# Attention visits in pairs of one window, with the score weighting on ScalarE and the one-hot made by one operation per visit

## The reference

```python
h = relu(layernorm(x))                       # x [12500, 64]
lin_x = h @ W_lin.T + b_lin
feat = concat([h[src], edge_attr, h[dst]])   # 144 per edge
scores = relu(feat @ W_att1.T + b_att1) @ W_att2.T + b_att2
m = segment_max(scores, src)                 # per source node
e = exp(scores - m[src])
denom = segment_sum(e, src)
msg = segment_sum(e / denom[src] * lin_x[dst], src)
# then a gated update (sigmoid, sigmoid, tanh) of every node with an edge
```

## Time and profile before

| what | us |
|---|---|
| median of three runs (lowest, highest) | 6971.01 (6955.53, 6972.53) |
| the profiled execution | 6953.3 |
| its span | 6951.5 |
| row send, first start of line 832 to last | 2519.9 to 4770.8 |
| attention, first C_N to the first operation after it | 4801.04 to 6833.62 |

### The profile page before, as it was taken

The page is one execution under the profiler, slowest core; times in us unless marked ns, Lnnn a source line. Parts: engine busy times, 40 slices in busy tenths (PEclk is TensorE's granted clock), DMA queues, the critical chain, the costliest instruction groups (busy, mean ns, idle before and its releaser), DMA issues.

```text
span 6951.5 us, 172751 instructions
## 1 busy us (share of the span) xinstructions
PE 4916.4 (71%) x30025; PEld 3702.1 (53%) x30026; DVE 4522.2 (65%) x20036; ACT 2115.2 (30%) x5541; POOL 4929.4 (71%) x10449
## 2 busy tenths in 40 slices
PE   6444777777545766676666666666888888888887
PEld 2334444444434544455445444444777777777775
DVE  5777888888434743333333333335999999999997
ACT  4000000000000432222222222223555555555555
POOL 1677777777777367777777777776777777777775
PEclk9555555555555777767877787776888888888888
DMA  8333333333333143333333333334333333333333
GB/s 270 67 60 60 57 60 60 57 60 60 64 60 61 62 133 111 111 110 109 105 106 105 106 106 105 106 105 128 95 94 94 95 95 95 94 94 95 95 95 93
DMA packets 1146496, 649.15 MB, mean 93 GB/s; under 512 B 798450, under 2 KB 1050340, under 8 KB 1145573
## 3 DMA queue, kind: packets, MB, share of 16 engines
q1 hardware_dynamic: 1006804, 412.21, 24.3%
q0 software_dynamic: 137728, 233.30, 11.8%
q10 hardware_dynamic: 1888, 2.83, 0.2%
HBM read 360.75 MB, written 311.42 MB: 97 GB/s over the span
## 4 chain that ended last, share of the span: by engine, by line
issue 19%; PE 15%; POOL 14%; DVE 8%; DMA 4%; ACT 3%; POOLq 1%; DVEq 1%; ACTq 0%; SPq 0%
PE banks L1397 7%; POOL rows_by_src L832 6%; DMA rows_by_src<-ring 3%; PE banks L1443 3%; DVE wide L1991 2%; DVE wide L1996 1%; DVE ring L2002 1%; ACT ring L1085 1%; ACT ring L1092 1%; POOL ring L893 1%; PE banks L1398 1%; PE banks L1385 1%; PE banks L1434 1%; DVE ring L1947 1%; PE banks L1458 1%
## 5 line engine op out<-in xcount | busy, mean ns | idle before, releaser
L832 POOL DMA_INDIRECT rows_by_src<-ring x1760 | 1711.7, 973 | 553.1 <-issue 488.5
L804 POOL DMA_INDIRECT wide<-msg_table,ring x1664 | 1578.8, 949 | 632.1 <-issue 419.4
L1397 PE MATMUL banks<-wide,ring 128*128 x3520 | 1281.9, 492 | 473.6 <-ACT ring L1085 403.4
L1311 PE MATMUL banks<-wide,ring 128*128 x3520 | 859.5, 426 | 505.7 <-DVE acc L1764 190.9
L1397 PEld LDWEIGHTS banks<-wide,ring 128*128 128x128 f32 x3520 | 742.5, 261 | 746.6 <-issue 696.2
L1311 PEld LDWEIGHTS banks<-wide,ring 128*128 128x128 f32 x3520 | 784.7, 328 | 584.0 <-issue 583.5
L1092 ACT COPY ring<-banks 128x416 f32<-128x416 f32 x880 | 402.2, 510 | 1448.8 <-PE banks L1398 1448.8
L1958 DVE COPY ring<-ring 128x4 f32<-128x4 f32 x440 | 80.1, 182 | 1145.5 <-DMA rows_by_src<-ring 1145.4
L1443 PE MATMUL banks<-wide,ring 128*128 x5328 | 708.6, 262 | 0.0
L1764 DVE TENSOR_TENSOR acc<-acc,banks 128x64 f32 x1760 | 388.8, 221 | 366.0 <-DVE acc L1764 201.8
L1443 PEld LDWEIGHTS banks<-wide,ring 128*128 128x128 bf16 x5328 | 544.1, 108 | 114.2 <-issue 0.2
(11 more groups left out here) (326 smaller groups left out, 9426.3 us busy)
## 6 DMA issues: line engine op xcount, KB each, us to landing
wide<-rows_by_src SPq DMA_DIRECT2D x1776, 105.0 KB, 2.0
ring<-attr_turned SPq DMA_DIRECT2D x440, 128.0 KB
attr_turned<-ring SPq DMA_DIRECT2D x416, 96.0 KB
rows_by_src<-ring POOLq DMA_INDIRECT x1760
wide<-msg_table,ring POOLq DMA_INDIRECT x1664
ring<-attr_by_dst SPq DMA_DIRECT2D x208, 64.0 KB
attr_turned<-ring SPq DMA_DIRECT2D x208, 64.0 KB
attr_by_dst<-in_edge_attr_dram SPq DMA_DIRECT2D x1, 13281.2 KB
```

What stands on the lines that cost most here:

```text
L804: g.indirect_dma_start(out=A_g[:, b * GV + u, :], out_offset=None, in_=table[:, :], in_offset=bass.IndirectOffsetOnAxis(ap=A_idx[:, b * GV ...
L832: g.indirect_dma_start(out=rows_d[:, :], out_offset=bass.IndirectOffsetOnAxis(ap=B_pos[:, s, u:u + 1], axis=0), in_=B_row[:, s, u, :], in_ ...
L1311: last = mm(bank[s][:, u * HID:(u + 1) * HID], A_D[:, s, u, :], A_g[:, ds(r[u], 1), :].rearrange("p a k -> p (a k)"), start=True, stop=True)
L1397: mm(b, B_DT[:, t, u, :], qh[:, w, :].rearrange("p a k -> p (a k)"), start=True, stop=False)
```

## The change

In the attention stage, the visits of a window are rounded up to an even number, so that two neighbours in a group of four (a pair) always have the same window. There are then 1,872 visits, 468 ticks, 78 bodies. The maximum, scan, penalty and split of the maximum run on 2 columns a tick, not 4; PE adds the sums of a pair in PSUM, and the DVE adds 2 sums a tick into `acc`, not 4. Penalties are made once ahead of the loop (`pens`), and POOL copies twelve of them each body.

C_N is made without C_kl: one DVE operation per visit adds the window's first node to the node numbers and compares with the edge's source, so four `tensor_scalar` of 128 columns with two per-partition scalars stand for one operation of 512. It stands behind the scan in DVE's tick. C_W goes from POOL (one operation of 260 columns) to ACT (four of 65, with a per-partition scale), behind the exponential. C_S and C_STb go to the end of ACT's tick, the turning of C_N behind the turning of the scores on PE.

In the rows stage, rows outside the window are sent to 2,048 spare rows behind the table, a place of its own for each, and the indirect DMA has no bounds check; the DVE has one small operation more per four visits.

```diff
-C_VISITS = C_BODY * -(-VISITS // C_BODY)
+C_VISITS = C_BODY * -(-(-(-N_EDGES // P) + N_WIN - 1 + N_WIN) // C_BODY)
 C_LOOPS = C_VISITS // C_BODY
-VTAB = max(VISITS, C_VISITS)
+PV = GV // 2
+VTAB = VISITS
 VCHUNK = VTAB // 4
...
-        rows_d = dram("rows_by_src", [SLOTS, ROW])
+        rows_d = dram("rows_by_src", [SLOTS + BODY * P, ROW])
...
-                            in_=B_row[:, s, u, :], in_offset=None, bounds_check=SLOTS - 1, oob_is_err=False).then_inc(b_sc[s], 16)
+                            in_=B_row[:, s, u, :], in_offset=None).then_inc(b_sc[s], 16)
...
-                if 0 in stages:
-                    n = i * C_BODY + s * GV
-                    pool.wait_ge(c_in[s], H0_LOADS[s] + 16 * GV * (i + 1))
-                    after_c(pool, c_N, s, i, CS)
-
-                    g.tensor_tensor(C_kl[:, s, :], C_V[:, s, :, ROW_SRC], wbase[:, ds(n, GV)], ALU.subtract).then_inc(c_kl, 1)
-
-                    m_pen = ch.do(g.tensor_tensor(C_pen[:, s, :], wbase_all[:, ds(n, GV)], wbase[:, ds(n, GV)], ALU.subtract))
+                if 0 in stages and s == 3:
+                        after_c(pool, c_new, CS - 1, i, CS)
+                        g.tensor_copy(C_pen, pens[:, ds(i * (CS * PV), CS * PV)]).then_inc(c_pen, 1)
                 if 2 in stages:
                     t, j = stages[2]
                     sp_ = [C_parts[:, t, k * GV:(k + 1) * GV] for k in range(PARTS)]
                     after_c(pool, c_s, t, j, incs=2)
                     after_c(pool, c_pt, t, j, CS)
-                    m_r = ch.do(g.tensor_tensor(C_r[:, t, :], C_s[:, t, :], sp_[0], ALU.subtract))
-                if 0 in stages:
-                    ch.need(m_pen)
-                    g.tensor_tensor(C_pen[:, s, :], C_pen[:, s, :], C_step, ALU.mult).then_inc(c_pen, 1)
-                if 2 in stages:
-                    ch.need(m_r)
+                    ch.link(g.tensor_tensor(C_r[:, t, :], C_s[:, t, :], sp_[0], ALU.subtract))
                     ch.link(g.tensor_tensor(sp_[1], C_r[:, t, :], C_zero, ALU.add))
                     g.tensor_tensor(sp_[2], C_r[:, t, :], sp_[1], ALU.subtract).then_inc(c_sp, 1)
                 if 4 in stages:
...
-                    after_c(pool, c_p, t, j)
-                    after_c(pool, c_ag, t, j, 2)
-                    g.tensor_tensor(C_W[:, t % 2, :, :], C_V[:, t, :, H1:ROW_SRC],
-                                    per_group(C_p[:, t, :], HID + 1), ALU.mult).then_inc(c_W, 1)
                 if 3 in stages:
                     t, j = stages[3]
...
                     after_c(pool, c_new, t, j)
+                    pool.wait_ge(c_pen, j + 1)
                     after_c(pool, c_mm, t, j, CS)
...
-            run_ticks(pool, tick, 5, ch, CS * (1 + 2 + 1 + 4), CS, C_LOOPS)
+            run_ticks(pool, tick, 5, ch, CS * (2 + 1 + 4), CS, C_LOOPS)
...
-                if 0 in stages:
-                    after_c(act, c_N, s, i)
-                    after_c(act, c_ag, s, i, CS)
-                    a.activation(C_S[:, s, :, :], C_N[:, s, :, :], ACT.Identity, bias=ones[:, 0:1], scale=-1.0).then_inc(c_S, 1)
                 if 4 in stages:
...
                     after_c(act, c_d, t, j)
                     after_c(act, c_W, t, j, CS)
                     a.activation(C_p[:, t, :], C_d[:, t, :], ACT.Exp).then_inc(c_p, 1)
-                if 0 in stages:
-                    after_c(act, c_St, s, i)
-                    after_c(act, c_mm, s, i, CS)
-                    a.activation(C_STb[:, s, :, :], four(bank_b[0], P), ACT.Identity, bias=ones[:, 0:1], scale=-1.0).then_inc(c_STc, 1)
+                    after_c(act, c_p, t, j)
+                    after_c(act, c_ag, t, j, 2)
+                    for u in range(GV):
+                        last = a.activation(C_W[:, t % 2, u, :], C_V[:, t, u, H1:ROW_SRC], ACT.Identity, scale=C_p[:, t, u:u + 1])
+                    last.then_inc(c_W, 1)
                 if 2 in stages:
                     t, j = stages[2]
                     after_c(act, c_pt, t, j)
                     after_c(act, c_MKt, t, j, 2)
                     a.copy(C_PT[0:PARTS * GV, t % 2, :], bank_b[1][0:PARTS * GV, 0:P]).then_inc(c_pc, 1)
+                if 0 in stages:
+                    after_c(act, c_N, s, i, incs=GV)
+                    after_c(act, c_ag, s, i, CS)
+                    a.activation(C_S[:, s, :, :], C_N[:, s, :, :], ACT.Identity, bias=ones[:, 0:1], scale=-1.0).then_inc(c_S, 1)
+                    after_c(act, c_St, s, i)
+                    after_c(act, c_mm, s, i, CS)
+                    a.activation(C_STb[:, s, :, :], four(bank_b[0], P), ACT.Identity, bias=ones[:, 0:1], scale=-1.0).then_inc(c_STc, 1)
...
-                    r = regs(ENG.PE, wwin, j1 * C_BODY + t1 * GV, N_WIN - 1)
+                    r = regs(ENG.PE, wpair_of, j1 * (C_BODY // 2) + t1 * PV, N_WIN - 1, PV)
...
-                        last = mm(bank[5][:, u * PARTS:(u + 1) * PARTS], C_STb[:, t, u, :], C_mp[:, t, u, :], start=True, stop=True)
+                        last = mm(bank[5][:, u * PARTS:(u + 1) * PARTS], C_STb[:, t, u, :], C_mp[:, t, u // 2, :], start=True, stop=True)
...
-                if 0 in stages:
-                    after_c(pe, c_N, s, i)
-                    after_c(pe, c_STc, s, i, 1)
-                    for u in range(GV):
-                        last = tr(bank_b[0][:, u * P:(u + 1) * P], C_N[:, s, u, :], ident_b[:, :])
-                    last.then_inc(c_St, 1)
                 if 1 in stages:
                     after_c(pe, c_STc, t1, j1)
                     after_c(pe, c_add, t1, j1, 1, incs=2)
...
-                        w = p_tab[:, ds(r[u], 1), :].rearrange("p a k -> p (a k)")
+                        w = p_tab[:, ds(r[u // 2], 1), :].rearrange("p a k -> p (a k)")
...
                     after_c(pe, c_pc, t, j, 1)
                     turn(pe, "pe")
                     tr(bank_b[1][0:PARTS * GV, 0:P], C_parts[:, t, :], ident_b[:, :]).then_inc(c_pt, 1)
+                if 0 in stages:
+                    after_c(pe, c_N, s, i, incs=GV)
+                    after_c(pe, c_STc, s, i, 1)
+                    for u in range(GV):
+                        last = tr(bank_b[0][:, u * P:(u + 1) * P], C_N[:, s, u, :], ident_b[:, :])
+                    last.then_inc(c_St, 1)
                 if 5 in stages:
                     t, j = stages[5]
                     after_c(pe, c_W, t, j)
                     after_c(pe, c_acc, t, j, 2)
                     after_c(pe, c_S, t, j)
                     for u in range(GV):
-                        last = mm(bank[6 + t % 2][:, u * (HID + 1):(u + 1) * (HID + 1)], C_S[:, t, u, :], C_W[:, t % 2, u, :],
-                                  start=True, stop=True)
+                        last = mm(bank[6 + t % 2][:, (u // 2) * (HID + 1):(u // 2 + 1) * (HID + 1)], C_S[:, t, u, :], C_W[:, t % 2, u, :],
+                                  start=u % 2 == 0, stop=u % 2 == 1)
                     last.then_inc(c_ag, 1)
...
-                v.tensor_tensor(nt[0:K, :], t1, hs, ALU.mult).then_inc(s_vcols, 1)
+                if k == 0:
+                    v.tensor_tensor(nt[0:K, :], t1, hs, ALU.mult).then_inc(s_vcols, 1)
+                else:
+                    ch.link(v.tensor_scalar(ei, t1, 1.0, None, ALU.add))
+                    ch.link(v.tensor_scalar(ei, ei, 1, None, ALU.arith_shift_right))
+                    ch.link(v.tensor_copy(t1, ei))
+                    v.scalar_tensor_tensor(nt[0:K, :], t1, 2.0, hs, ALU.mult, ALU.mult).then_inc(s_vcols, 1)
...
-                    ch.link(v.scalar_tensor_tensor(B_sh[:, s, :], B_rec[:, s, :, 1], -BIG, B_in[:, s, :], ALU.add, ALU.mult))
+                    ch.link(v.tensor_tensor(B_sh[:, s, :], B_rec[:, s, :, 1], aside[:, s, :], ALU.subtract))
+                    ch.link(v.tensor_tensor(B_sh[:, s, :], B_sh[:, s, :], B_in[:, s, :], ALU.mult))
                     if not first(i):
                         dve.wait_ge(b_sc[s], 16 * GV * i)
                     v.tensor_copy(B_row[:, s, :, ROW_SRC], B_rec[:, s, :, 0]).then_inc(b_pos, 1)
-                    v.tensor_scalar(B_pos[:, s, :], B_sh[:, s, :], BIG, None, ALU.add).then_inc(b_pos, 1)
+                    v.tensor_tensor(B_pos[:, s, :], B_sh[:, s, :], aside[:, s, :], ALU.add).then_inc(b_pos, 1)
...
-            v.memset(C_step, MASKED / P).then_inc(c_init, 1)
+            dve.wait_ge(c_init, N_CINIT - 1)
+            ch.link(v.tensor_tensor(pens, of_pairs(wbase_all[:, 0:C_VISITS]), of_pairs(wbase), ALU.subtract))
+            v.tensor_scalar(pens, pens, MASKED / P, None, ALU.mult).then_inc(c_init, 1)
...
-                if 0 in stages:
-                    after_c(dve, c_kl, s, i)
-                    after_c(dve, c_MKt, s, i, CS)
-                    after_c(dve, c_S, s, i, CS)
-                    v.tensor_tensor(C_N[:, s, :, :], iota_b[:, :].unsqueeze(1).to_broadcast([P, GV, P]),
-                                    per_group(C_kl[:, s, :], P), ALU.not_equal).then_inc(c_N, 1)
                 if 6 in stages:
```

(29 more changed lines are left out.)

77 lines of the change are left out of this document (44 added, 33 removed).

## The result

The changed kernel takes 7185.29 us (median of 4 runs, 7180.22 to 7193.27) against 6971.77 of before: a ratio of 1.0313, 95% interval 1.0294 to 1.0331. It is slower, as forecast, but by 213.5 us and not by the forecast 79; the time lies above the range that was given. In the profiled execution the span is 7177.8 us against 6951.5, 226.3 more.

What follows compares the result with a forecast made beforehand. It took a closed ACT-POOL loop, 4.60 us a tick with POOL's hold-up, as the attention stage's new bound: +135, rows stage -48, one-time work +3, so +90 us, said as 7050 (6985 to 7135; 8 in 10: 6910 to 7160).

Steps and rivals of the forecast that it cites:

- ACT-POOL: Attention stage: closed loop of ACT's queue and POOL's answer, score copy to next score copy, 4.57 us, the new bound.
- self wait: ACT, attention stage: C_W waits for the exponential's own result, taken as 0.10 us, from 0.05 to 0.20.
- I add 0.03, and keep 0 to 0.4: Attention stage: us a tick added to the loop because DVE's C_N can hold up POOL's operations behind the score split.
- 3.96 us busy at most, and less than that: PE, attention stage: same number of matmuls, so 3.96 us a tick at most, less from start to start.
- done some 1.5 us before ACT comes to them: PE, attention stage: turnings of scores and C_N finish about 1.5 us early, so ACT's late operations need not wait.
- the rows stage's -48: Rows stage: the send without bounds check takes the gather's 1.248 us a step, not 1.277; -48 us taken.
- Rival D: Rows stage: no gain, forecast without the -48, 7098 us; counted within the forecast's 0.60 chance.
- Forecast tick 4.60: Attention stage: loop of 4.57 plus 0.03 for C_N's hold on POOL; 468 ticks make 2,152.8 us, +135.
- B: Attention stage: the loop is a little shorter, tick 4.3 to 4.4 us, 6920 to 6967 us in all; chance 0.11.
- A: Attention stage: the DVE sets the tick, 4.05 us with waits; -168 us in sum, 6803 us; chance 0.19.
- C: Attention stage: POOL held up through all of C_N, tick 4.95 to 5.0 us, about 7210 us; chance 0.10.
- The forecast's 3.95 for the DVE: DVE's tick, attention stage: 3.19 us left plus 0.76 for four tensor_scalar, 3.95 us, between 3.71 and 4.35.

Runs made afterwards that it cites:

- e3: Changed kernel with the DVE's C_N at the head of its tick instead of behind the scan: 7058.36 us, ratio 1.0140 to the kernel before.
- e11: Changed kernel with C_N at the head of DVE's tick and six extra turnings a tick on PE: 7071.07 us, ratio 1.0143.
- e4: Changed kernel with six extra turnings of a constant on PE while it waits for C_N: 7135.41 us, ratio 1.0251.
- e8: Changed kernel with C_N behind the scan but in its old form, one tensor_tensor of 512 columns from POOL's C_kl: 7225.45 us, ratio 1.0367.
- e2: Changed kernel with C_S a tick later, where ACT waited for POOL's clip: 7179.52 us, ratio 1.0318.
- e1: Changed kernel with the bounds check put back on the rows stage's send: 7192.68 us (one run).
- e5: Changed kernel with both moves, C_N at the head of DVE's tick and C_S a tick later in the trip to POOL: 6839.49 us, ratio 0.9816.
- e9: Changed kernel with C_S a tick later in the trip to POOL and six extra turnings a tick on PE: 6943.59 us, ratio 0.9959.

## Why the prediction was right and wrong

**Right: the closed loop and its sum.** The forecast had 4.57 us for ACT-POOL. e3 and e11, in which no tick is longer than 4.65, measure 4.567 and 4.560; the shortest tick of the changed kernel is 4.55. Member by member, on average in e11: score copy to exponential 1.98 (1.93 forecast), C_W 0.97 (0.94), exponential to C_W 0.27 (0.31 with the self wait), the copy 0.15 (0.16), C_S 0.62 (0.63), C_STb 0.57 (0.60). The members miss by up to 0.05 in both directions and cancel; that the sum is right to 0.01 is partly luck.

**Right: what the profile would show.** The score copy hardly waits for the DVE, the exponential is where ACT waits, the DVE is 86% busy (under 88% forecast). These two groups of the changed kernel, 5400 to 6800, answer to the second of the earlier trace rows: 1.48 us a tick for POOL's clip (1.3 forecast), 0.05 for the scores.

```profile
L1103 ACT ACTIVATE ring<-ring,b2bc 128x4 bf16<-128x4 f32 x292 | 83.6, 286 | 17.1 <-DVE wide L2004 15.9
...
L1112 ACT ACTIVATE ring<-ring 128x4 f32<-128x4 f32 x292 | 60.3, 206 | 432.8 <-POOL ring L872 432.8
```

**Wrong: "I add 0.03, and keep 0 to 0.4" for C_N's hold on POOL.** In the changed kernel it is 0.07 us a tick, by the trip to POOL against e11's, and 0.153 where the clock is held up (e4 less e11), 72 us in 468. The bounds held it, the value taken did not. The reading behind it (one operation stretched in the earlier trace rows, none in the earlier trace rows) was of a C_N that stood at the head of the tick, mostly outside the trip. Its own sentence, that C_N would now fall on the operations behind the score split, was the better guide. The Trainium skill's rule that was weighed there (SBUF — State Buffer, "Who interferes with whom") is borne out in direction: e8's unbroken operation kept POOL out to its end, 0.68 us for 0.20, and beside the four parts POOL's operation took 0.29. Whether the four parts enter the mode that the rule speaks of, no run here shows.

**Wrong: PE "3.96 us busy at most, and less than that", and its turnings "done some 1.5 us before ACT comes to them".** That took the clock for constant and looked for no second path. In the tick at 6002.83 the 1.5 us hold. But the move of C_N behind the scan put PE's turning, and by PE's order its sums and masks, into a loop with the DVE, and that loop is 5.59 us at the low clock; there the turning ends at 5669.90, and C_STb starts at 5669.97. e4 puts the changed kernel's loss from it at 0.097 a tick over the stage, 45 us, or more if the added matmuls cost time too. It also hid the fact that ACT-POOL is not the only bound: without e2 the forecast's cause would have passed for the whole one.

**Wrong: the rows stage's -48.** It is -2.6. The step that failed is that the 0.029 us between gather and send were put down to the bounds check; the check costs about 0.009 (e1), and without it the send still takes 1.278 us a step against the gather's 1.25. Rival D, a part of the forecast's own range, said this.

**The size.** Forecast tick 4.60, measured 4.801 over the whole stage. 0.20 over 468 ticks is 94 us; with the 45 that the rows stage did not give, the forecast's +90 becomes 229, against 226.3 in the span. The 0.20 cannot be shared out cleanly. Run by run over the whole stage, e11 has 4.551, e4 0.153 more for C_N's place, and the changed kernel another 0.097 for the clock; read in the changed kernel's own window, C_N's hold on POOL is 0.07 and the waits for the DVE and PE 0.15.

**The range.** It did not follow from its own terms. A loop of 4.80 us and no gain in the rows stage, both within what the forecast counted as itself, give 6953.3 + 228 + 3 = 7185. The range stopped at 7135, and the wider one at 7160. That corner is what came. In B, 6920 to 6967 is reckoned from the median and not from the profile, as it says; from the profile it would be 6903 to 6950.

**The rivals.** A, the DVE decides: not in this kernel, but e5 shows it once both loops are open: shortest tick 3.94, mean 4.075, the DVE 98% busy. The forecast's 3.95 for the DVE is met by luck: C_N takes 1.03 us and not 0.76, and the rest 2.91 and not 3.19. B failed with its 4.3 to 4.4. C named the time within 25 us and the mechanism in part: POOL is held up, by 0.07 to 0.15 and not through the whole of C_N.

**What stays open.** Why e3's clock stays at 0.78 with PE 86% busy while e5's is 0.97 with PE 83% busy, and how the low clock and PE's waits feed each other, is only seen side by side here, not taken apart. Why the send without a check is slower than the gather stays open too.

## What to carry to other kernels

When no engine is full, list every closed loop through the engines' queues, not only the longest: here one was 4.57 us and the next at most 4.08 or 5.59, by the clock, and cutting the first alone gained nothing, both together 346 us. Count a loop that runs through PE at the low clock too, and try a few throw-away matmuls as a probe: if they raise the granted clock and make the kernel faster, PE at the low clock has a part in what sets it. Place an operation by what waits behind it in its queue, not by its length: C_W cost ACT 0.97 us a tick and was still worth 211 to 377 us away from POOL.

## What was not expected of the hardware

- Six matmuls a tick whose result is thrown away raised the granted clock from 0.77 to 0.99 (e4) and from 0.73 to 0.99 (e9), and made the kernel 50 and 236 us faster (43 and 250 by the ratios).
- Four `tensor_scalar` of 128 columns with two per-partition scalars, f32 to bf16, start 0.26 us apart (1.03 from the first to the next operation), 0.07 above the value taken.
- A bounds check on an indirect DMA with nothing out of bounds costs about 0.009 us an instruction (15.4 us in 1,760, one trace).
